# RWKV mixing plus Hadamard feed-forward layer: the first pair's recurrence items spread over three stretches, weights split ahead of W2's loads

## The chip, the cores and the metric

The kernel runs on one core of one Trainium2 chip. The metric is the device time of one execution in microseconds, the median of three; lower is better. The engines are named as in the profile: PE is the matrix engine and PEld its weight loads, DVE the vector engine, ACT the activation engine, POOL the GpSimd engine, SP the engine whose queue (SPq) issues every DMA here. They run side by side, each in program order, and meet at semaphores.

## The reference

`x` is 4 x 2048 tokens of 512 channels, float32. The kernel computes `out = x + attn(xn) + ffn(xn)` with `xn = layernorm(x)`. Cut to what matters:

```
shifted = xn one token later (zero at t = 0)
xq = mu_q * xn + (1 - mu_q) * shifted                for q in k, v, r
k, v, r = xk @ Wk.T, xv @ Wv.T, xr @ Wr.T            (512 x 512 each)
per channel, over t:  p  = max(pp, u + k_t);  e1 = exp(pp - p);   e2 = exp(u + k_t - p)
                      y  = (e1*aa + e2*v_t) / (e1*bb + e2)
                      p2 = max(w + pp, k_t);  e1b = exp(w + pp - p2);  e2b = exp(k_t - p2)
                      aa, bb, pp = e1b*aa + e2b*v_t, e1b*bb + e2b, p2      (w = -exp(wkv_w))
attn = (sigmoid(r) * y) @ Wo.T
ffn  = fwht(silu(xn @ W1.T) * (xn @ W3.T)) @ W2.T    (hidden size 2048; fwht: Walsh-Hadamard, / sqrt(2048))
```

## The kernel before

**Tiling.** The 8192 tokens are eight **pairs** `s` of two halves (a and b) of 512 tokens. Every product is done in three matmuls (high by high, low by high, high by low) on operands that were split into a high part (an ACT copy) and a low part (a subtraction). The low parts of activations are made on DVE, those of weights on POOL. The fwht is folded into W2 once, in the prologue.

**A pair** has an up stage and a down stage. The up stage is 16 steps `j`. A step makes 7 "pieces" of 6 matmuls (L852, L854, L855; a seven-product scheme for both halves and W1, W3), and from step 1 on 12 matmuls of half a's down projection (L862 to L864), 24 in steps 5, 8 and 10. The down stage is 24 steps `n`. PE runs 12 matmuls of the next pair's k, v, r product for each (L934 to L936, `r_unit` n), from n = 4 on behind 12 of half b's down projection (`down_b` n - 4). ACT and DVE at step n prepare the mixed input of `r_unit` n + 3 (L1014, L1355, L1026, L1364) and half b's hidden tile n - 1, and at n = 1 and 2 DVE empties the four accumulators of half a (`add_residual`, L1580), which `down_b` 0 needs. `turn` lies between the stages.

**The recurrence** has 8 items a pair (two halves, four channel tiles). Item w needs its k and v tile, and goes through stages 0, 1, 3, 4, 5, 6, 7 on DVE (`wkv`, L1401 on): 0 and 1 are a copy, a scan and two exponent arguments, then ACT makes two rectified and two exponentiated tiles (`rectified`, `exponentials`), 3 to 5 are products, scans and sums, 6 is a reciprocal, 7 ends in the attention tile `attf`. Items run one after the other, since the carry goes from tile half to tile half and they share `z`, `e`, `pab`, `attf`. In the up stage slot `3 j + slot` (three slots a step, `recurrence`) runs stage `divmod(3 j + slot, 8)[1]` of item 1 to 6, so 48 slots for six items, in every pair. Item 7 runs at down steps 3 to 10, the next pair's item 0 at down steps 11 to 18. In the prologue item 0 of the first pair runs around `r_unit` 8 and 9.

**DVE in an up step j**, in this order: `hidden_a(j-1)` (L1482, frees the bank of piece 5 of step j), slot 0, `gate_a_added` (L1487), `gate_b_applied` (L1496), `hidden_b` (L1501), slot 1, `hidden_a_lo` (L1464), slot 2, the next pair's `normalisation`, `b_added` (L1505, L1507), `gate_a_applied` (L1491).

**The prologue and the first pair** are special. Weights come raw from HBM into 8 slots (`load_raws`, in the order of RAWS), ACT makes their high part (`split_high`), POOL their low part (`lo`, L733), SP stores the split weights to HBM (`store_split`) for the other seven pairs. In the first pair's up stage POOL also forms the sums of W1 and W3 (L746 to L751). The prologue loads W2 in four pieces of 1 MB (`load_w2`), turns it by Hadamard matmuls within tiles after `r_unit` 8 (L966) and across tiles after `r_unit` 14 (L947), and ACT copies each turned tile. For the first pair, the token means and 1/std are laid out over partitions by matmuls of diagonals (`make_diagonal` on DVE, L1315; `spread_tokens`, L955).

Of the kernel before, what the change touches and what calls it, by code (L numbers as in the profile page):

```python
# [116 lines left out]
def build(nc, x, x_t, w_units, vectors, hadamard, out):  # L117
# [15 lines left out]
    with ctx:  # L133
# [219 lines left out]
        def _(sp):  # L353
# [145 lines left out]
            def first_half(s, j):  # L499

                if j == 0 and not is_last(s):
                    load_rows(s + 1, 0)
                if j == 1 and not is_first(s):
                    store_out(s - 1, 1)
                if not is_last(s):
                    if j in (2, 4, 6):
                        load_rows(s + 1, j // 2)
                    if 2 <= j < 2 + KT:
                        load_columns(s + 1, j - 2)
                    if j in (6, 10):  # L510
# [5 lines left out]
                if j in (11, 14):  # L516
                    store_att_b(s, (j - 11) // 3)
# [32 lines left out]
            def down_step(s, n):  # L550

                if n == 0:
                    store_hidden_b(s, FT - 1)
                    if is_first(s):
                        for i in range(HIDB):
                            load_hidden_b(s, i)
                if n == 1:
                    store_att_b(s, 2)
# [19 lines left out]
                if n == 4:  # L578
                    store_out(s, 0)
                if n == 12:  # L580
                    store_att_b(s, 3)
# [106 lines left out]
            load_raws(RAW_AT["d", 1])  # L688
# [310 lines left out]
        def _(act):  # L999
# [114 lines left out]
            def split_high(unit):  # L1114
# [18 lines left out]
                act.activation(split_place(unit)[:, 0, :], split_source(unit), ACT.Copy).then_inc(split_hi, 1)  # L1133

            def up_step(s, j):
                first = is_first(s)

                step_w, at = divmod(3 * j + 2, 8)
                starts = 2 - (at - 1) if 1 <= at <= 3 else None
                w = 1 + step_w  # L1140
                if j == 0 or j == 1:
# [57 lines left out]
            def down_step(s, n):  # L1199

                with_r, with_d = not is_last(s), not (isinstance(s, int) and s < 0)
                r = s + 1
                if with_r:
                    if n % KT == KT - 1:
                        evacuate(r, n // KT)
                    if n + MIX_AHEAD < R_UNITS:
                        mix_second(r, n + MIX_AHEAD)
                    if n + MIX_AHEAD + 1 < R_UNITS:
                        mix_first(r, n + MIX_AHEAD + 1)
                if with_d:  # L1210
                    if 1 <= n < 1 + ND:
                        hidden_b_hi(s, n - 1)
                    if n == WKV_LAST_AT + 1:
                        rectified(s, 7)
                    if n == WKV_LAST_AT + 2:
                        exponentials(s, 7)
                if with_r:
                    if with_d and n == WKV_FIRST_AT + 1:
                        rectified(r, 0)
                    if with_d and n == WKV_FIRST_AT + 2:  # L1220
                        exponentials(r, 0)
# [13 lines left out]
            split_high(("r", 2))  # L1235
            mix_second(0, 0)
            mix_second(0, 1)
            mix_first(0, 2)
            mix_second(0, 2)
            mix_first(0, 3)  # L1240
            for n in range(R_UNITS):
# [12 lines left out]
                if n == PASS_TWO_AFTER:  # L1254
                    act.wait_ge(half_stored, 16 * W2_LOADS)
                    for k, i in enumerate(TILES_TURNED):
                        act.wait_ge(w2_psum, FT + k + 1)
                        act.activation(fly[1][:, i, :], acc[i % TT][:, :], ACT.Copy).then_inc(w2_copied, 1)
                if n + 3 >= R_UNITS:
                    split_high(("u", 0, n + 3 - R_UNITS))  # L1260
# [11 lines left out]
        def _(dve):  # L1272
# [37 lines left out]
            def make_diagonal(h, a):  # L1310

                if h:
                    dve.wait_ge(spread, a + 1)
                for t in range(TT):
# [195 lines left out]
            def recurrence(s, j, slot):  # L1510

                w_item, stage = divmod(3 * j + slot, 8)
                wkv(s, 1 + w_item, stage)

# [67 lines left out]
            def down_step(s, n):  # L1582

                with_r, with_d = not is_last(s), not (isinstance(s, int) and s < 0)
                r = s + 1
                if not with_d and n == PASS_ONE_AFTER + 1:
                    for stage in range(3, 7):
                        wkv(r, 0, stage)
                if not with_d and n == 3:
                    dve.wait_ge(rstd_ready, 2)  # L1590
                    make_diagonal(1, 1)
                if with_r:
# [9 lines left out]
                if with_r:  # L1602
                    centre_at, scale_at = (CENTRE_AT, SCALE_AT) if with_d else (FIRST_CENTRE_AT, FIRST_SCALE_AT)
# [4 lines left out]
                if with_d and 0 <= n - WKV_LAST_AT < 8:  # L1608
                    wkv(s, 7, n - WKV_LAST_AT)
                if with_r:  # L1610
                    if with_d and 0 <= n - WKV_FIRST_AT < 8:
                        wkv(r, 0, n - WKV_FIRST_AT)
                    if not with_d and n == PASS_ONE_AFTER:
                        wkv(r, 0, 0)
                        wkv(r, 0, 1)
                    if not with_d and n == PASS_ONE_AFTER + 4:
                        wkv(r, 0, 7)
                    made_at, low_at = (MADE_AT, LOW_AT) if with_d else (FIRST_MADE_AT, FIRST_LOW_AT)
                    for i in made_at.get(n, ()):
# [14 lines left out]
            def first_stats(h):  # L1634
# [5 lines left out]
                add_eps(0, h)  # L1640
                dve.wait_ge(mean_copied, h + 1)
                dve.wait_ge(had_loaded, 16)
                make_diagonal(h, 0)

            first_stats(0)
            dve.wait_ge(vec_loaded, 16)
            dve.tensor_scalar(one_less_mu[:, :, :], vec[:, 0:3, :], -1.0, 1.0, ALU.mult, ALU.add)\
# [79 lines left out]
```

## Time and profile before

| | us |
|---|---|
| median of 3 runs | 2746.8 (2746.8 to 2746.91) |
| profiled execution | 2745.27, of which the span is 2743.5 |
| PE busy | 2672.6 (97%), granted clock 0.994 of full |
| DVE busy | 2204.7 (80%) |
| PEld / ACT / POOL busy | 2185.4 (80%) / 1317.5 (48%) / 238.2 (9%) |
| chain that ended last | PE 88%, DVE 8%, ACT 2%, issue 1%, DMA 1% |

All of the POOL's work and nearly all of PE's idle time lie before 404 us, in the prologue and in the first pair. A row of the timeline gives start, duration, engine, line, operation, output, inputs and, in brackets, the idle time of the engine before it and what ended it. A matmul of 512 columns starts 0.227 us after the one before it at the full clock, though its row shows a duration of 0.39.

### The profile page before, as it was taken

To read this page: it belongs to the slowest core of one execution; us is meant where nothing else is said; L and a number is where in the kernel's file an instruction comes from. 1 tells how busy PE (TensorE), PEld (TensorE's weight loads), DVE (VectorE), ACT (ScalarE), POOL (GpSimd) and SP (SyncE) were. 2 spreads that over 40 slices of the span, in tenths; PEclk is the share of its full clock that TensorE was granted. 3 is DMA by queue.
4 is the path that set the end of the run, shared out by engine and by line. 5 is a ranking of instruction groups with operands and counts; after the bars stand their busy time and mean duration, and the time that the engine had idled before them with its cause. 6 is when DMAs were issued, how large, how long until landed. Compare 5 with 4: busy or idle time off the path is not lost.

```text
span 2743.5 us, 33882 instructions
## 1 busy us (share of the span) xinstructions
PE 2672.6 (97%) x11616; PEld 2185.4 (80%) x11616; DVE 2204.7 (80%) x2970; ACT 1317.5 (48%) x2107; POOL 238.2 (9%) x180
## 2 busy tenths in 40 slices
PE   7988899999999999999999999999999999999999
PEld 4666678888888888888888888888888888888887
DVE  7698988788887888788886888878888688877785
ACT  5655456444554445444454444644455444554442
POOL 2287830000000000000000000000000000000000
PEclk9999999999999999999999999999999999999999
DMA  6787678787877878787786877878787786876777
GB/s 222 293 283 234 230 248 276 239 273 221 276 250 255 259 232 271 240 277 241 246 280 218 271 251 248 279 238 275 222 269 260 246 272 219 275 245 221 229 227 271
DMA packets 244951, 691.50 MB, mean 252 GB/s; under 512 B 31920, under 2 KB 31920, under 8 KB 244272
## 3 DMA queue, kind: packets, MB, share of 16 engines
q1 hardware_dynamic: 244784, 689.34, 76.2%
q8 instruction: 96, 1.57, 0.2%
q14 instruction: 71, 0.58, 0.1%
HBM read 575.94 MB, written 113.30 MB: 251 GB/s over the span
## 4 chain that ended last, share of the span: by engine, by line
PE 88%; DVE 8%; ACT 2%; issue 1%; DMA 1%; POOL 0%; ACTq 0%; DVEq 0%
PE gamma L852 12%; PE gamma L855 12%; PE gamma L854 12%; PE acc L862 10%; PE acc L864 10%; PE acc L863 10%; PE gamma L934 4%; PE gamma L936 4%; PE gamma L935 4%; PE alpha L852 2%; PE alpha L855 2%; PE alpha L854 2%; PE alpha L936 1%; PE alpha L935 1%; PE alpha L934 1%
## 5 line engine op out<-in xcount | busy, mean ns | idle before, releaser
L1048 ACT ACTIVATE step<-gamma 128x512 f32<-128x512 f32 x512 | 306.2, 598 | 837.8 <-PE gamma L855 814.2
L852 PE MATMUL gamma<-xs_high,wring 128*128 128x512 f32 x1280 | 502.4, 393 | 29.7 <-DVE step L1482 20.6
L855 PE MATMUL gamma<-xs_low,wring 128*128 128x512 f32 x1280 | 500.7, 391 | 0.0
L854 PE MATMUL gamma<-xs_high,wring 128*128 128x512 f32 x1280 | 500.7, 391 | 0.0
L862 PE MATMUL acc<-vring,hid 128*128 128x512 f32 x1232 | 482.0, 391 | 9.4 <-POOL vring L733 4.4
L863 PE MATMUL acc<-vring,hid 128*128 128x512 f32 x1232 | 480.0, 390 | 0.0
L864 PE MATMUL acc<-vring,hid 128*128 128x512 f32 x1232 | 479.8, 389 | 0.0
L852 PEld LDWEIGHTS gamma<-xs_high,wring 128*128 128x128 f32 x1280 | 241.7, 189 | 85.8 <-issue 22.6
L862 PEld LDWEIGHTS acc<-vring,hid 128*128 128x128 f32 x1232 | 231.9, 188 | 64.0 <-issue 11.2
L855 PEld LDWEIGHTS gamma<-xs_low,wring 128*128 128x128 f32 x1280 | 241.8, 189 | 50.8
L854 PEld LDWEIGHTS gamma<-xs_high,wring 128*128 128x128 f32 x1280 | 242.0, 189 | 49.8
L1355 DVE SCALAR_TENSOR_TENSOR step<-xt,vec,step 128x512 f32<-128x512 f32 x192 | 144.3, 755 | 160.3 <-ACT step L1014 159.5
L864 PEld LDWEIGHTS acc<-vring,hid 128*128 128x128 f32 x1232 | 231.6, 188 | 48.4
L863 PEld LDWEIGHTS acc<-vring,hid 128*128 128x128 f32 x1232 | 231.9, 188 | 47.8
L1026 ACT ACTIVATE mix<-step 128x512 fp32r<-128x512 f32 x192 | 120.6, 629 | 254.7 <-PE gamma L936 216.6
L1443 DVE RECIPROCAL z<-z 128x512 f32<-128x512 f32 x64 | 214.1, 3345 | 0.0
L934 PE MATMUL gamma<-mix,wring 128*128 128x512 f32 x522 | 203.8, 390 | 3.9 <-DVE mix L1364 3.9
L936 PE MATMUL gamma<-mix,wring 128*128 128x512 f32 x522 | 203.6, 390 | 0.0
L935 PE MATMUL gamma<-mix,wring 128*128 128x512 f32 x522 | 203.6, 390 | 0.0
L727 POOL TENSOR_TENSOR mean_rstd<-var_eps,half 128x4 f32<-128x4 f32 x16 | 22.7, 1416 | 1883.5 <-DVE var_eps L1302 1883.5
L1487 DVE TENSOR_TENSOR step<-step,alpha 128x512 f32<-128x512 f32 x128 | 86.4, 675 | 112.4 <-PE alpha L855 101.3
L1364 DVE TENSOR_TENSOR mix<-step,mix 128x512 fp32r<-128x512 f32 x192 | 139.0, 724 | 18.4 <-ACT mix L1026 9.9
(170 smaller groups left out, 4770.1 us busy)
## 6 DMA issues: line engine op xcount, KB each, us to landing
wring<-u_split SPq DMA_DIRECT2D x336, 512.0 KB, 4.3
vring<-d_split SPq DMA_DIRECT2D x288, 512.0 KB, 4.3
wring<-r_split SPq DMA_DIRECT2D x168, 512.0 KB, 4.2
raw<-spilled SPq DMA_DIRECT2D x160, 256.0 KB, 4.2
spilled<-step SPq DMA_DIRECT2D x128, 256.0 KB, 4.3
wlast<-u_split SPq DMA_DIRECT2D x112, 256.0 KB, 3.4
u_split<-wring SPq DMA_DIRECT2D x48, 512.0 KB, 3.1
res<-x SPq DMA_DIRECT2D x16, 1024.0 KB, 7.7
```

Source lines behind the costliest of these rows:

```text
L852: pe.matmul(bank[:, :], w[:, 0, col], high, start=fresh and kt == 0, stop=False, skip_group_check=True)
L854: pe.matmul(bank[:, :], w[:, 1, col], high, start=False, stop=False, skip_group_check=True)
L855: last = pe.matmul(bank[:, :], w[:, 0, col], low, start=False, stop=kt == 1, skip_group_check=True)
L862: pe.matmul(acc[tt][:, :], a[:, 0, col], w[:, 0, :], start=first, stop=False)
L863: pe.matmul(acc[tt][:, :], a[:, 1, col], w[:, 0, :], start=False, stop=False)
L864: return pe.matmul(acc[tt][:, :], a[:, 0, col], w[:, 1, :], start=False, stop=final)
L934: pe.matmul(bank[:, :], w[:, 0, col], m_in[:, 0, :], start=kt == 0, stop=False)
L935: pe.matmul(bank[:, :], w[:, 1, col], m_in[:, 0, :], start=False, stop=False)
L936: last = pe.matmul(bank[:, :], w[:, 0, col], m_in[:, 1, :], start=False, stop=kt == KT - 1)
L1048: act.activation(to, bank[:, :], ACT.Copy).then_inc(u_copied, 1)
L1355: dve.scalar_tensor_tensor(f, xt[:, kt, 1 + h * N:1 + (h + 1) * N], vec[:, q, kt:kt + 1], f, ALU.mult, ALU.add).then_inc(mix_full, 1)
L1443: dve.reciprocal(z[:, 1, :], z[:, 1, :]).then_inc(wkv_step, 1)
```

## The change

What it does, in six parts:

1. Up stage of the first pair only: the slot table becomes FIRST_UP_WKV. It holds stage 7 of item 1 and all of items 2 to 5, 34 slots of 48, with free slots between. The other pairs' tables give the same order as before.
2. Down stage of the first pair: FIRST_DOWN_WKV runs item 6 at n = 0 to 6, item 7 at n = 7 to 13, the next pair's item 0 at n = 15 to 22. The next pair's `centre` and `scale` move from n = 3 to 6 to n = 4 to 7, the stores of attention tiles of half b to j = 12 and n = 0, 8, 14.
3. Prologue: item 1 is run too; stages 0 and 1 at `r_unit` step 13, stages 3 to 6 at step 15 ahead of that step's mixing, its ACT work among the copies of W2's second turn.
4. ACT in the first pair rectifies and exponentiates where the new tables have stage 1, always in slot 1 or 2.
5. Raw k, v, r weights: all 12 loads are issued ahead of W2's four loads (the last four wait for a freed slot). ACT splits them two at a time: r3 to r5 before the first `r_unit`, r6 to r11 by step 2.
6. The second half's diagonals are made by eight ACT copies with a scale at step 1, no longer by DVE; their matmuls come after `r_unit` 4 in place of 3.

```diff
-WKV_LAST_AT, WKV_FIRST_AT = 3, 11
+UP_WKV = {k: (1 + k // 8, k % 8) for k in range(3 * FT)}
+FIRST_UP_WKV = {2: (1, 7)}
+FIRST_UP_WKV |= {k: (2, i) for i, k in enumerate((3, 5, 6, 8, 9, 11, 13, 15))}
+FIRST_UP_WKV |= {16 + i: (3, i) for i in range(8)}
+FIRST_UP_WKV |= {k: (4, i) for i, k in enumerate((24, 25, 27, 28, 30, 31, 33, 34))}
+FIRST_UP_WKV |= {k: (5, i) for i, k in enumerate((36, 37, 39, 40, 42, 43, 45, 46))}
+DOWN_WKV = {3 + i: ((7, i),) for i in range(8)} | {11 + i: ((8, i),) for i in range(8)}
+FIRST_DOWN_WKV = {0: ((6, 0), (6, 1)), 2: ((6, 3),), 3: ((6, 4),), 4: ((6, 5),), 5: ((6, 6),), 6: ((6, 7),),
+                  7: ((7, 0), (7, 1)), 9: ((7, 3),), 10: ((7, 4),), 11: ((7, 5),), 12: ((7, 6),), 13: ((7, 7),),
+                  15: ((8, 0),), 16: ((8, 1),), 18: ((8, 3),), 19: ((8, 4),), 20: ((8, 5),), 21: ((8, 6),),
+                  22: ((8, 7),)}
+RECTIFY_AT, EXP_AT = {4: 7, 12: 8}, {5: 7, 13: 8}
+FIRST_RECTIFY_AT, FIRST_EXP_AT = {0: 6, 7: 7, 16: 8}, {1: 6, 8: 7, 17: 8}
-SPREAD_AFTER, PASS_ONE_AFTER, PASS_TWO_AFTER = 3, 8, 14
+SPREAD_AFTER, PASS_ONE_AFTER, PASS_TWO_AFTER = 4, 8, 14
...
             load_columns_first(0)
-            load_raws(2)
+            load_raws(4)
             load_rows_first(2)
             load_rows_first(3)
-            load_raws(4)
-            load_w2(0)
+            load_raws(RAW)
             load_columns_first(1)
-            load_raws(6)
-            load_w2(1)
-            load_raws(RAW)
-            load_w2(2)
-            load_w2(3)
+            load_raws(12)
+            for i in range(W2_LOADS):
+                load_w2(i)
...
+            def diagonals_b(a):
+                if a:
+                    act.wait_ge(rstd_ready, 2)
+                else:
+                    act.wait_ge(mean_copied, 2)
+                act.wait_ge(spread, 2)
+                for t in range(TT):
+                    act.activation(diagonal[:, a, t, :], had[:, 2, :], ACT.Copy, scale=mean_rstd[:, 1, a, t:t + 1])\
+                        .then_inc(diagonal_made, 1)
...
             for n in range(R_UNITS):
                 down_step(-1, n)
-                if n + 3 < 12:
-                    split_high(("r", n + 3))
+                if n < 3:
+                    split_high(("r", 6 + 2 * n))
+                    split_high(("r", 7 + 2 * n))
+                if n == 1:
+                    diagonals_b(0)
+                    diagonals_b(1)
...
-                if not with_d and n == PASS_ONE_AFTER + 1:
+                if not with_d and n in (PASS_ONE_AFTER + 1, PASS_TWO_AFTER + 1):
                     for stage in range(3, 7):
-                        wkv(r, 0, stage)
-                if not with_d and n == 3:
-                    dve.wait_ge(rstd_ready, 2)
-                    make_diagonal(1, 1)
+                        wkv(r, int(n > PASS_TWO_AFTER), stage)
```

## Rows read from the trace of the kernel before

**Rows 1.** Busy time by engine in stretches (busy, instructions; clock, DMA share, GB/s).
```profile
128.98:380.03 251.05, 216.41 (x888) 170.94 (x889) 227.59 (x238) 127.36 (x220) 191.37 (x143) 0.96 0.71 246
...
404.00:510.00 106.00, 105.98 (x468) 87.76 (x468) 81.21 (x105) 53.96 (x85) 0.00 (x0) 1.00 0.78 253
510.00:711.00 201.00, 201.00 (x888) 166.42 (x887) 168.69 (x240) 90.11 (x143) 2.86 (x2) 1.00 0.78 254
```

**Rows 2.** PE's waits, 128.98 to 404 us: for whom, total us, times, longest.
```profile
PE gamma L852 <- DVE step L1482: 20.6, 7, 5.3
PE acc L862 <- POOL vring L733: 4.4, 3, 1.7
PE gamma L852 <- ACT step L1048: 4.2, 4, 2.4
PE gamma L852 <- POOL wring L733: 4.0, 4, 1.7
PE gamma L934 <- DVE mix L1364: 3.9, 1, 3.9
```

**Rows 3.** PE's timeline: its longest stalls in the first pair (idle time in brackets).
```profile
180.82 0.47 PE L852 MATMUL gamma<-xs_high,wring 128*128 128x512 f32 x1 [2.40 <-ACT step L1048]
...
208.74 0.77 PE L852 MATMUL gamma<-xs_high,wring 128*128 128x512 f32 x1 [3.61 <-DVE step L1482]
209.30 0.63 PE L854 MATMUL gamma<-xs_high,wring 128*128 128x512 f32 x1
...
258.69 0.77 PE L852 MATMUL gamma<-xs_high,wring 128*128 128x512 f32 x1 [5.27 <-DVE step L1482]
...
344.14 0.77 PE L852 MATMUL gamma<-xs_high,wring 128*128 128x512 f32 x1 [5.18 <-DVE step L1482]
...
386.89 0.47 PE L934 MATMUL gamma<-mix,wring 128*128 128x512 f32 x1 [3.85 <-DVE mix L1364]
```

**Rows 4.** DVE's timeline: the recurrence's first item, in the prologue.
```profile
55.05 0.16 DVE L1417 COPY pab<-carry 128x3 f32<-128x3 f32 x1
...
66.80 0.69 DVE L1427 TENSOR_TENSOR z<-e,kvr 128x512 f32<-128x512 f32 x1 [8.96 <-ACT e L1095]
...
73.15 3.35 DVE L1443 RECIPROCAL z<-z 128x512 f32<-128x512 f32 x1
...
85.58 0.69 DVE L1457 SCALAR_TENSOR_TENSOR attf<-kvr,z 128x512 f32<-128x512 f32 x1
```

**Rows 5.** DVE's timeline: `hidden_a` that opens and that follows up step 7.
```profile
239.36 0.69 DVE L1482 TENSOR_TENSOR step<-step,gamma 128x512 f32<-128x512 f32 x1
...
257.86 0.69 DVE L1482 TENSOR_TENSOR step<-step,gamma 128x512 f32<-128x512 f32 x1
```

**Rows 6.** Groups by line and form, DVE, 129 to 380 us (POOL at work).
```profile
L1501 DVE TENSOR_TENSOR step<-step 128x512 f32<-128x512 f32 x15 | 14.5, 967 | 1.6
```

**Rows 7.** The same group in the second pair, 510 to 711 us (POOL idle).
```profile
L1501 DVE TENSOR_TENSOR step<-step 128x512 f32<-128x512 f32 x15 | 10.4, 692 | 1.6
```

**Rows 8.** Busy time as in Rows 1, of up steps 2 and 7 alone.
```profile
155.80:170.33 14.53, 12.93 (x55) 10.09 (x56) 14.32 (x17) 6.45 (x12) 12.15 (x10) 1.00 0.90 311
...
235.43:248.48 13.05, 12.62 (x56) 10.02 (x56) 12.91 (x13) 7.08 (x13) 12.97 (x10) 1.00 1.00 359
```

**Rows 9.** Timelines of PE, DVE: around the turns of W2 in the prologue.
```profile
50.76 1.75 DVE L1364 TENSOR_TENSOR mix<-step,mix 128x512 fp32r<-128x512 f32 x1
...
53.70 15.70 PE L966 MATMUL acc<-fly,had 128*128 128x512 f32 x32 [3.33 <-DVE xt L1341]
...
105.68 0.75 DVE L1355 SCALAR_TENSOR_TENSOR step<-xt,vec,step 128x512 f32<-128x512 f32 x1 [15.54 <-ACT step L1014]
```

**Rows 10.** DVE's timeline: down steps 1 and 2 of the first pair.
```profile
398.35 0.75 DVE L1355 SCALAR_TENSOR_TENSOR step<-xt,vec,step 128x512 f32<-128x512 f32 x1 [4.45 <-ACT step L1014]
...
403.28 1.28 DVE L1580 TENSOR_TENSOR res<-res,acc 128x512 f32<-128x512 f32 x2
```

**Rows 11.** DVE's waits, 404 to 510 us.
```profile
DVE step L1355 <- ACT step L1014: 16.0, 13, 3.2
```

More of the change, by code:

```diff
@@ L515, in first_half @@
                     load_residual(s, 0)
-                if j in (11, 14):
+                if j == 12 if is_first(s) else j in (11, 14):
                     store_att_b(s, (j - 11) // 3)
@@ L556, in down_step @@
                             load_hidden_b(s, i)
-                if n == 1:
+                if n == 0 and is_first(s):
+                    store_att_b(s, 1)
+                if n == (8 if is_first(s) else 1):
                     store_att_b(s, 2)
@@ L579, in down_step @@
                     store_out(s, 0)
-                if n == 12:
+                if n == (14 if is_first(s) else 12):
                     store_att_b(s, 3)
@@ L1133, in split_high @@
                 act.activation(split_place(unit)[:, 0, :], split_source(unit), ACT.Copy).then_inc(split_hi, 1)
+            def diagonals_b(a):
[7 more added lines that the diff above has]
+                        .then_inc(diagonal_made, 1)
             def up_step(s, j):
                 first = is_first(s)
-                step_w, at = divmod(3 * j + 2, 8)
-                starts = 2 - (at - 1) if 1 <= at <= 3 else None
-                w = 1 + step_w
+                starts = w = None
+                for slot in range(3):
+                    item, stage = (FIRST_UP_WKV if first else UP_WKV).get(3 * j + slot, (0, 0))
+                    if stage == 1:
+                        starts, w = slot, item
                 if j == 0 or j == 1:
@@ L1212, in down_step @@
                         hidden_b_hi(s, n - 1)
[L1213 to L1216, printed above, removed]
+                    rectify_at, exp_at = (FIRST_RECTIFY_AT, FIRST_EXP_AT) if is_first(s) else (RECTIFY_AT, EXP_AT)
+                    for at, what in ((rectify_at, rectified), (exp_at, exponentials)):
+                        if at.get(n) == 8:
+                            if with_r:
+                                what(r, 0)
+                        elif n in at:
+                            what(s, at[n])
                 if with_r:
[L1218 to L1221, printed above, removed]
                     high_at = HIGH_AT if with_d else FIRST_HIGH_AT
@@ L1236, in _ @@
             mix_second(0, 0)
+            split_high(("r", 3))
             mix_second(0, 1)
             mix_first(0, 2)
+            split_high(("r", 4))
             mix_second(0, 2)
             mix_first(0, 3)
+            split_high(("r", 5))
             for n in range(R_UNITS):
                 down_step(-1, n)
-                if n + 3 < 12:
-                    split_high(("r", n + 3))
+                if n < 3:
[4 more added lines that the diff above has]
+                    diagonals_b(1)
                 if n == PASS_ONE_AFTER:
@@ L1258, in _ @@
                         act.activation(fly[1][:, i, :], acc[i % TT][:, :], ACT.Copy).then_inc(w2_copied, 1)
+                        if k == 3:
+                            rectified(0, 1)
+                        if k == 9:
+                            exponentials(0, 1)
                 if n + 3 >= R_UNITS:
@@ L1310, in make_diagonal @@
             def make_diagonal(h, a):
-                if h:
-                    dve.wait_ge(spread, a + 1)
                 for t in range(TT):
@@ L1510, in recurrence @@
             def recurrence(s, j, slot):
-                w_item, stage = divmod(3 * j + slot, 8)
-                wkv(s, 1 + w_item, stage)
+                at = FIRST_UP_WKV if is_first(s) else UP_WKV
+                if 3 * j + slot in at:
+                    wkv(s, *at[3 * j + slot])
             def normalisation(r, j):
@@ L1602, in down_step @@
                 if with_r:
-                    centre_at, scale_at = (CENTRE_AT, SCALE_AT) if with_d else (FIRST_CENTRE_AT, FIRST_SCALE_AT)
+                    late = not with_d or is_first(s)
+                    centre_at, scale_at = (FIRST_CENTRE_AT, FIRST_SCALE_AT) if late else (CENTRE_AT, SCALE_AT)
                     if n in centre_at:
@@ L1607, in down_step @@
                         scale(r, 1, scale_at[n])
-                if with_d and 0 <= n - WKV_LAST_AT < 8:
-                    wkv(s, 7, n - WKV_LAST_AT)
+                if with_d:
+                    for item, stage in (FIRST_DOWN_WKV if is_first(s) else DOWN_WKV).get(n, ()):
+                        if item < 8:
+                            wkv(s, item, stage)
+                        elif with_r:
+                            wkv(r, 0, stage)
                 if with_r:
-                    if with_d and 0 <= n - WKV_FIRST_AT < 8:
-                        wkv(r, 0, n - WKV_FIRST_AT)
                     if not with_d and n == PASS_ONE_AFTER:
@@ L1617, in down_step @@
                         wkv(r, 0, 7)
+                    if not with_d and n == PASS_TWO_AFTER - 1:
+                        wkv(r, 1, 0)
+                        wkv(r, 1, 1)
                     made_at, low_at = (MADE_AT, LOW_AT) if with_d else (FIRST_MADE_AT, FIRST_LOW_AT)
@@ L1640, in first_stats @@
                 add_eps(0, h)
-                dve.wait_ge(mean_copied, h + 1)
-                dve.wait_ge(had_loaded, 16)
-                make_diagonal(h, 0)
             first_stats(0)
+            dve.wait_ge(mean_copied, 1)
+            dve.wait_ge(had_loaded, 16)
+            make_diagonal(0, 0)
             dve.wait_ge(vec_loaded, 16)
```

## The prediction

> **What bounds the kernel now.** I read the stretches first. In the second pair's up stage 888 matmuls take 201 us and PE has no idle time; the first pair runs the same 888 in 251.05, with PE busy for 216.41 and the granted clock at 0.96; its down stage, 404 to 510, has no gap left [rows 1]. So what PE loses lies before 404 us, and whatever PE wins there moves the end by as much. At 0.2266 us a matmul the up stage would take 201.2, so 49.8 us are lost in it. PE's waits name them [rows 2]: 20.6 for DVE's L1482 in 7 waits, 8.4 for POOL's weight splits, 4.2 for ACT's copies, and 3.9 for DVE's mixing at the turn. The rest is clock: after each of the longest stalls [rows 3] matmuls start 0.43 us apart (209.30 is such a one) for a while before they come back to 0.227. Summing what start to start exceeds 0.2266, that cost 2.6 us after the stall at 208.74, 1.6 after 258.69, 1.3 after 293.29, 1.7 after 344.14 and 1.7 after 386.89.
>
> The reader is to see why L1482 is late. It is the first DVE instruction of step j and frees the bank of PE's fourth piece. DVE is busy for 227.59 of 251.05 us [rows 1]. From one L1482 to the next in step 7 it works 18.5 us without a gap [rows 5], against 54 matmuls or 12.24 us of PE. Two things fill it: recurrence stages (5, 6 and 7 of an item here), and POOL, beside which a 0.692 us instruction takes 0.967 [rows 6, 7].
>
> **Up stage, the recurrence.** An item is 15 DVE instructions with 14.3 us between them (first, one of the middle and last in [rows 4]), 13.7 with the overlap at each handover. By that timeline stages 0 and 1 take 1.35 each, 3 and 4 1.8, 5 2.4, 6 3.3 and 7 1.4. Before, 6 items or 82 us lie in the 16 steps; after, 4 items and a stage 7, or 56. What counts is where. The seven stalls for L1482 come at j = 2, 3, 5, 8, 10, 12 and 13 (those at 5, 8 and 13 stand in [rows 3], the one at 10 is like them), most behind a heavy step. Slot by slot, recurrence work goes at j = 1 from 6.1 to 2.7, at 2 from 6.2 to 1.8, at 4 from 7.6 to 3.3, at 9 from 6.1 to 1.8, at 12 from 7.6 to 2.7. Steps 5 to 8 keep what they had (7.1 at j = 7), and j = 3, 11 and 14 get more (by 1.2, 1.6 and 0.7). PE needs L1482 about 4.8 us into the step, which is the slack. So I take away the stalls at j = 2 and 3 (0.4 and 0.9), 5 (3.6), 10 (3.9), 12 (1.4) and 13 (5.2): 15.4 us, with 5.6 of clock behind 5, 10 and 13. The one at j = 8 (5.27 and 1.6 of clock) I leave: before step 6 DVE already waits for PE, so its lateness at 8 grows inside steps 6 and 7, which the change does not touch.
>
> **ACT.** The stall of 2.40 at 180.82 [rows 3] is an ACT copy queued behind `rectified`, which waited 3.4 us for DVE's stage 1. The new table has no stage 1 in slot 0, so ACT never takes it up early in a step; with the one of 1.2 before it, whose cause is DVE's lateness in step 2, 3.6 us go.
>
> **Turn.** The stall of 3.85 at 386.89 with 1.7 of clock [rows 3] comes from DVE's lateness in step 15, which loses stage 5 (3.1 as it ran there). Pairs without it show no wait. 5.6 go.
>
> **POOL** works 191.37 us in these 16 steps [rows 1], 12.0 a step, nearly what PE needs (12.6). Where PE stood still for DVE, POOL caught up; that cover goes. The 8.4 us of waits on it are bounded by none left (gain 8.4) and by 12 steps that last as long as step 2, 14.5 us, in place of about 13.3, near step 7 [rows 8], the common length of steps without a DVE stall (loss 14.4). I take a loss of 2, near the common length, since DVE also asks for less beside it. What DVE and POOL do to each other is 0.967 against 0.692 [rows 6, 7]. The Trainium skill says of this (SBUF — State Buffer, Who interferes with whom) that a vector instruction with two SBUF inputs and a GpSimd instruction that reads SBUF exclude each other for the whole instruction. By that rule each removed two-input stage frees POOL as well; this is the rival "more goes" below, and the sum stands without it.
>
> **Down stage.** Item 6 adds 13.7 us of DVE between n = 0 and 6. DVE waits 16.0 us for ACT there in 13 waits [rows 11] and is busy 81 of 106 [rows 1], so the sum fits. The start does not quite: stages 0 and 1 fit into the idle 4.45 before 398.35 [rows 10], but ACT's two rectified tiles (1.9 us) then stand ahead of the mix of n = 1 and its two exponentials (2.0) ahead of the mix of n = 2. DVE's `add_residual` pair, now at 403.28 [rows 10], comes some 2.4 later, and `down_b` 0 waits for it with 0.25 to spare now. Bounds: 0, and 3.9 if all of ACT's work shows. I take 2.1. Queued behind on SP: stores of attention tiles at n = 0, 8 and 14, a step or more after their stage 7, so SP does not stand.
>
> **Prologue.** Splits done early on ACT and POOL take POOL's share out of DVE's chain to `scale` (the 1.75 at 50.76 against 0.69 [rows 9], four such), which ends PE's wait of 3.33 at 53.70. Against it, `r_unit` 4 follows 3 directly, without the diagonals' matmuls to cover the copying of four banks, and ACT gets there behind eight diagonals and four splits. I see `r_unit` 5 start where it did and the turn start between 0 and 3 us earlier; I take 2. Diagonals leave DVE (1.7 us), covered by the same wait. W2's loads leave SP some 12 us later, are needed at 53.70, and 4 MB at the 246 GB/s of [rows 1] take 17 us, so they land by 44; cost 0, and one for one beyond 53.7. Item 1: stages 3 to 6 are 9.6 us of DVE that start when ACT's exponentials end, near 99, in the idle 15.54 before 105.68 [rows 9]. They reach to 108, 2.5 beyond; DVE has 1 us of idle from there to the first pair's start, so that is 1.5 later. Bounds 0 and 2.5. Together 0.5 gained, between 3 gained and 2.5 lost.
>
> **The sum.** 15.4 + 5.6 + 3.6 + 5.6 + 0.5 - 2 - 2.1 = 26.6 us. The profiled execution took 2745.27 (1.8 of it outside the span), so 2718.7; the median of the runs lies 1.5 above it, so **2720.2**.
>
> **The rivals.**
> - The split chain sets the pace: PE runs ahead, and POOL, or the transfers behind it, end each step. For: step 7 at 13.05 us had POOL busy 12.97 and the DMA share at 1.00 [rows 8]. Against: it was still just 0.8 above 12.24. With the 14.4 us worked out above in place of 2: 2732.6. Chance 0.23.
> - More goes: the stall at j = 8 too (6.9) and half of POOL's waits, as DVE and POOL hinder each other less. For: [rows 6, 7]. Against: steps 6 and 7 are untouched. 26.6 + 6.9 + 2 + 4 = 39.5 less: 2707. Chance 0.17.
> - Nothing comes of it: the DMA engines, at 0.71 of their time over the stage [rows 1] and full in step 7, already hold it at 246 GB/s, and PE waits for raw weights instead of DVE. 2746. Against: no wait of PE or of ACT's splits ends in a load. Chance 0.05.
> - Slower: DVE never catches up in the first down stage, since its idle time there (16.0 [rows 11]) is ACT's lateness and cannot be used. It decides if the delay of n = 2 comes again in each of the 20 steps: 2.1 x 20 = 42 lost against 28.7 won, 2760. Against: a step there lasts 5.44 us and mixing is three ahead. Chance 0.03.
>
> **How the numbers follow.** The forecast has 0.52. The range takes in the first two rivals with their unknown terms, 2705 to 2735, and leaves the other two out. About 0.2%, 5.5 us, is what a measurement can tell from no change: faster 0.92, same 0.05, slower 0.03.
>
> **What would show it.** Right: PE's waits for DVE's L1482 fall to one long one of 5 us, at j = 8; none of 3 us at the turn; up stage 223 to 228 us long; POOL's waits as now or somewhat more; a new PE wait for L1580 near the start of the down stage; the first pair starts within 2 us of 128.98; the second pair's up stage still 201. Wrong: more than 15 us of waits for POOL, waits for loads, or new L1482 stalls at j = 12 or 15.

## The result, and the profile after

The changed kernel took **2727.5 us** (2726.2 to 2728.8) against 2746.9 of the kernel before beside it: ratio 0.9929, 95% interval 0.9917 to 0.9941. The forecast was 2720.2, its range 2705 to 2735. The gain is 19.4 us where 26.6 were forecast, so the direction and the range held and 7.2 us of the gain are missing. The profiled execution has a span of 2724.8 us. Because lines moved, the old L1482 is now L1514, L852 L863, L862 L873, L1048 L1059, L733 L744, L934 L945, L1364 L1396, L1580 L1613, L1505 L1537; the high split on ACT is L1144.

Busy time by engine in four stretches of the changed kernel, columns as in [rows 1]: the up stage of the first pair; from its end to the first matmul of the next `r_unit`; from there to the second pair; the second pair's up stage.

```profile
129.95:359.60 229.65, 209.60 (x888) 167.65 (x889) 211.09 (x216) 119.66 (x211) 193.75 (x143) 0.98 0.77 266
359.60:363.86 4.26, 3.05 (x14) 2.23 (x13) 4.26 (x7) 3.61 (x6) 1.69 (x1) 1.00 0.91 350
363.86:493.60 129.74, 125.02 (x547) 102.25 (x547) 106.05 (x138) 68.75 (x107) 0.00 (x0) 1.00 0.75 252
...
505.00:706.00 201.00, 201.00 (x888) 166.38 (x887) 171.41 (x244) 87.25 (x141) 2.86 (x2) 1.00 0.80 257
```

The same cuts of the kernel before:

```profile
380.03:386.89 6.86, 3.01 (x12) 2.17 (x13) 6.86 (x11) 2.65 (x5) 1.70 (x1) 1.00 0.66 242
386.89:512.95 126.06, 125.81 (x547) 103.63 (x548) 93.54 (x123) 65.63 (x104) 0.00 (x0) 0.99 0.77 253
```

The ledger from these rows: the first pair starts 1.0 us later (129.99 against 128.98), the up stage is 21.4 shorter (251.05 in [rows 1], 229.65 here), the turn 2.6 shorter, and the same 547 matmuls of the down stage and the last step before the second pair take 3.7 longer. Sum 19.3. From there on the two kernels are nearly alike: the second pair's up stage is 201.00 in both, and the whole spans differ by 18.7. Two other cuts are used below. Between PE's first matmul into `alpha` in step 0 and the one in step 15, "from `alpha` to `alpha`", the up stage took 236.1 before and 217.0 now; from the latter to the second pair's first `alpha` it took 145.1 in both.

PE's waits in the changed kernel, 127 to 400 us (for whom, total us, times, longest), to be read against [rows 2]:

```profile
PE gamma L863 <- DVE step L1514: 8.3, 4, 5.2
PE acc L873 <- POOL vring L744: 6.7, 3, 3.6
PE acc L873 <- DVE res L1613: 3.6, 2, 1.9
PE gamma L863 <- POOL wring L744: 2.9, 4, 1.6
PE gamma L863 <- ACT step L1059: 2.0, 3, 1.4
...
PE gamma L945 <- DVE mix L1396: 1.2, 1, 1.2
PE gamma L945 <- DMA wring<-r_split: 0.8, 1, 0.8
```

The wait for `hidden_a` fell from 20.6 to 8.3. Those for POOL rose from 8.4 to 9.6, and the one for `add_residual` went from 0.25 in one wait to 3.6 in two. PE's timeline of the changed kernel has them in place; after none of them but the two at 215 and 248 does the clock fall for longer than a few matmuls:

```profile
215.09 0.71 PE L873 MATMUL acc<-vring,hid 128*128 128x512 f32 x1 [3.55 <-POOL vring L744]
...
248.79 0.76 PE L863 MATMUL gamma<-xs_high,wring 128*128 128x512 f32 x1 [5.22 <-DVE step L1514]
...
363.86 0.47 PE L945 MATMUL gamma<-mix,wring 128*128 128x512 f32 x1 [1.21 <-DVE mix L1396]
...
380.57 0.47 PE L873 MATMUL acc<-vring,hid 128*128 128x512 f32 x1 [1.77 <-DVE res L1613]
...
384.03 0.50 PE L873 MATMUL acc<-vring,hid 128*128 128x512 f32 x1 [1.85 <-DVE res L1613]
```

The one at 248.79 is the stall of step 8 that the prediction left in place; in [rows 3] it is the one at 258.69. The one at 215.09 is new, and the wait is put down to POOL. ACT's and POOL's timelines show who was late:

```profile
208.70 1.06 ACT L1100 ACTIVATE e<-z 128x1024 f32<-128x1024 f32 x1 [2.80 <-DVE z L1455]
209.67 1.04 ACT L1101 ACTIVATE e<-z 128x1024 f32<-128x1024 f32 x1
210.62 1.99 ACT L1106 ACTIVATE e<-e 128x1024 f32<-128x1024 f32 x2
212.51 0.57 ACT L1059 ACTIVATE step<-gamma 128x512 f32<-128x512 f32 x1
212.99 1.13 ACT L1144 ACTIVATE vring<-raw 128x512 fp32r<-128x512 f32 x2
```

```profile
210.14 1.02 POOL L738 TENSOR_TENSOR mean_rstd<-var_eps,half 128x4 f32<-128x4 f32 x1 [0.31 <-DVE var_eps L1336]
213.68 2.51 POOL L744 TENSOR_TENSOR vring<-raw,vring 128x512 fp32r<-128x512 f32 x2 [2.52 <-ACT vring L1144]
```

ACT waits 2.80 us at the rectified tiles of item 3, whose stage 1 DVE has only just made, then does the two rectified and two exponentiated tiles, and the split of the next `vring` tiles stands behind. POOL, idle for 2.52, cannot form the low part before that, and PE waits for it. So "waits for POOL" is here a wait for ACT's queue, and through it for DVE. Item 3's stage 1 stands in the same slot as in the kernel before, slot 2 of step 5; there PE had just stood 3.61 us for DVE [rows 3], ACT took item 3's tiles up without a wait at 217.11, and PE's wait for the next `vring` was 1.35.

### The profile page after: what moved, and what is told of

Its sections match the earlier page's. It is cut to its first block, busy times and chain, and to the rows that moved or that the text cites. A ratio compares the mean times of both kernels' runs of the same rounds, so it can differ in the third digit from the quotient of the medians.

```text
span 2724.8 us, 33882 instructions
## 1 busy us (share of the span) xinstructions
PE 2665.6 (98%) x11616; PEld 2181.7 (80%) x11616; DVE 2205.9 (81%) x2962; ACT 1318.0 (48%) x2115; POOL 243.0 (9%) x180
## 4 chain that ended last, share of the span: by engine, by line
PE 87%; DVE 8%; ACT 2%; issue 2%; DMA 1%; POOL 1%; SPq 0%; ACTq 0%; DVEq 0%
PE gamma L863 12%; PE gamma L865 12%; PE gamma L866 12%; PE acc L873 10%; PE acc L875 10%; PE acc L874 10%; PE gamma L945 4%; PE gamma L947 4%; PE gamma L946 4%; PE alpha L866 2%; PE alpha L865 2%; PE alpha L863 2%; PE alpha L946 1%; PE alpha L947 1%; PE alpha L945 1%
## 5 line engine op out<-in xcount | busy, mean ns | idle before, releaser
L1059 ACT ACTIVATE step<-gamma 128x512 f32<-128x512 f32 x512 | 305.7, 597 | 840.9 <-PE gamma L866 817.9
L863 PE MATMUL gamma<-xs_high,wring 128*128 128x512 f32 x1280 | 500.2, 391 | 14.2 <-DVE step L1514 8.3
L873 PE MATMUL acc<-vring,hid 128*128 128x512 f32 x1232 | 481.5, 391 | 14.2 <-POOL vring L744 6.7
L863 PEld LDWEIGHTS gamma<-xs_high,wring 128*128 128x128 f32 x1280 | 240.9, 188 | 69.3 <-issue 11.2
L873 PEld LDWEIGHTS acc<-vring,hid 128*128 128x128 f32 x1232 | 231.3, 188 | 68.9 <-issue 14.8
L1387 DVE SCALAR_TENSOR_TENSOR step<-xt,vec,step 128x512 f32<-128x512 f32 x192 | 144.4, 756 | 145.3 <-ACT step L1025 144.6
L945 PE MATMUL gamma<-mix,wring 128*128 128x512 f32 x522 | 204.0, 391 | 7.0 <-ACT kvr L1052 3.5
L1396 DVE TENSOR_TENSOR mix<-step,mix 128x512 fp32r<-128x512 f32 x192 | 135.9, 708 | 18.8 <-DMA spilled<-step 9.5
```

The costliest lines, as they stand in the source:

```text
L863: pe.matmul(bank[:, :], w[:, 0, col], high, start=fresh and kt == 0, stop=False, skip_group_check=True)
L873: pe.matmul(acc[tt][:, :], a[:, 0, col], w[:, 0, :], start=first, stop=False)
L945: pe.matmul(bank[:, :], w[:, 0, col], m_in[:, 0, :], start=kt == 0, stop=False)
L1059: act.activation(to, bank[:, :], ACT.Copy).then_inc(u_copied, 1)
L1387: dve.scalar_tensor_tensor(f, xt[:, kt, 1 + h * N:1 + (h + 1) * N], vec[:, q, kt:kt + 1], f, ALU.mult, ALU.add).then_inc(mix_full, 1)
```

## The experiments

**1. Which part carries the gain.** The recurrence tables alone, with the prologue's loads, splits and diagonals as before:

```diff
-            load_raws(4)
+            load_raws(2)
             load_rows_first(2)
             load_rows_first(3)
-            load_raws(RAW)
+            load_raws(4)
+            load_w2(0)
...
-                if n == 1:
-                    diagonals_b(0)
-                    diagonals_b(1)
```

> The recurrence part alone: the new tables of the first pair, item 1 in the prologue, the new stores; raw loads, splits and diagonals of the prologue as in the kernel before. Theory (the gain is the up stage's, from DVE's load per step): nearly the whole gain, 2728 to 2731 us, the up stage (first alpha piece of step 0 to that of step 15) at 217 us as with both parts. Rival (the prologue part carries a gain of its own of 5 us or more): 2733 or above.

Measured: 2728.1 (2726.3 to 2729.1), ratio 0.9935, interval 0.9918 to 0.9951, as the theory said. The up stage took 218.6 from `alpha` to `alpha`, and both long stalls of the changed kernel are there, 3.55 for `vring` and 5.28 for `hidden_a`. The other half, the prologue alone with the old tables:

```diff
-UP_WKV = {k: (1 + k // 8, k % 8) for k in range(3 * FT)}
-FIRST_UP_WKV = {2: (1, 7)}
+WKV_LAST_AT, WKV_FIRST_AT = 3, 11
...
-                if not with_d and n in (PASS_ONE_AFTER + 1, PASS_TWO_AFTER + 1):
+                if not with_d and n == PASS_ONE_AFTER + 1:
```

> The prologue part alone: k, v, r weights loaded and split ahead, diagonals of the second half on ACT, spread after r_unit 4; the recurrence as in the kernel before. Theory: PE starts W2's first turn about 1.2 us earlier (52.5 against 53.7) and, without item 1 behind W2's second turn, the first pair 1 to 3 us earlier; up stage 236 us as before; 2744 to 2746 us. Rival (the parts need each other): no gain or a loss, 2747 or above, since the copy of four banks behind r_unit 3 stalls PE by 3.5 us.

Measured: 2743.8 (2742.1 to 2745.0), ratio 0.9992, interval 0.9982 to 1.0001: no difference from the kernel before that the runs can tell. PE waits seven times for `hidden_a`, 18.8 us in all, as before; the first pair's pieces on the `alpha` bank begin at 128.25 in place of 131.68. In the whole change they begin at 131.46, with the tables alone at 134.61. So the tables carry the gain. The prologue's loads, splits and diagonals together win 3.2 to 3.4 us up to this point, and item 1's work there costs 2.9 to 3.2: together 0.2.

**2. The stall at 215.** Stages 0 and 1 of item 3, and with them the last of item 2, go one slot earlier, so that stage 1 is made sooner; stages 3 to 7 stay:

```diff
-FIRST_UP_WKV |= {k: (2, i) for i, k in enumerate((3, 5, 6, 8, 9, 11, 13, 15))}
-FIRST_UP_WKV |= {16 + i: (3, i) for i in range(8)}
+FIRST_UP_WKV |= {k: (2, i) for i, k in enumerate((3, 5, 6, 8, 9, 11, 13, 14))}
+FIRST_UP_WKV |= {k: (3, i) for i, k in enumerate((15, 16, 18, 19, 20, 21, 22, 23))}
```

> The changed kernel, with stage 7 of item 2 one slot earlier (step 4, slot 2), stages 0 and 1 of item 3 one slot earlier each (step 5, slots 0 and 1); stages 3 to 7 of item 3 stay. Theory (the new stall of 3.55 us for POOL's vring at 215 is ACT, which at the end of step 5 waits 2.8 us for the exponent arguments and then makes four tiles ahead of the weight split): that stall falls under 1 us, 2 to 3.5 us faster than the changed kernel, and the stall of 5.2 us at step 8 stays. Rival (POOL's own rate sets it): the stall at 215 stays within 1 us.

Measured: 2727.6 (2722.7 to 2730.9), ratio 0.9931, interval 0.9915 to 0.9948. Timelines of PE and ACT:

```profile
200.73 0.47 PE L863 MATMUL gamma<-xs_high,wring 128*128 128x512 f32 x1 [1.17 <-DVE step L1514]
...
215.24 0.47 PE L873 MATMUL acc<-vring,hid 128*128 128x512 f32 x1 [1.35 <-POOL vring L744]
...
207.62 1.06 ACT L1100 ACTIVATE e<-z 128x1024 f32<-128x1024 f32 x1 [0.22 <-DVE z L1455]
```

ACT's wait for item 3 fell from 2.80 to 0.22, and 3.55 became 1.35, the wait that the kernel before had there. So ACT's lateness made the other 2.2. The forecast was under 1 for the stall and 2 to 3.5 us for the kernel; neither came. A wait of 1.17 appeared ahead of it, in step 5, which got 1.4 us longer. Steps 5 and 6 together still got 2.3 shorter, of which 1.7 is lower clock behind the old stall. Over the whole stage, 216.6 from `alpha` to `alpha`, it is 0.4: steps 7, 10 and 11 came out longer and step 13 shorter, and the last three did so in a second execution of the changed kernel too (experiment 4).

**3. The stall at step 8.** As in 2, and stages 3 to 6 of item 3 also one slot earlier, so that step 7 loses stage 5 to step 6 and keeps 6 and 7:

```diff
-FIRST_UP_WKV |= {k: (3, i) for i, k in enumerate((15, 16, 18, 19, 20, 21, 22, 23))}
+FIRST_UP_WKV |= {k: (3, i) for i, k in enumerate((15, 16, 17, 18, 19, 20, 21, 23))}
```

> As s1_early, and stages 3, 4 and 5 of item 3 in step 6, stage 6 and 7 in step 7, so that step 7 has 4.7 us of recurrence in place of 7.1. Theory (the stall at step 8 is DVE's load inside step 7): the stall of 5.2 us for L1514 with its 1.9 us of slow clock falls under 2 us, and the kernel is 5 to 10 us faster than the changed one, 2718 to 2723. Rival (DVE and POOL are both full over steps 6 to 8, so the lateness only moves): stall of 4 us or more at step 7 or 8, under 4 us gained.

Measured: 2723.5 (2720.3 to 2724.0), ratio 0.9917, interval 0.9901 to 0.9934. The forecast was 2718 to 2723, and its rival wanted a stall of 4 us or more and under 4 us gained; the result lies between them, 4.0 us under the changed kernel by the medians. The four times, at most 2724.0, lie below all eight that the changed kernel took here and in experiment 4, at least 2726.2. The 5.22 at step 8 is gone, and in PE's timeline one of half its size stands a step earlier:

```profile
232.10 0.49 PE L863 MATMUL gamma<-xs_high,wring 128*128 128x512 f32 x1 [2.50 <-DVE step L1514]
```

The up stage took 212.2 from `alpha` to `alpha`, 4.8 us less. Of the three kernels of experiment 4 with the same tables, two took 212.2 and 212.3 and one 215.7, so how much of the 4.8 is the order's is known only roughly. Some of DVE's lateness in steps 6 to 8 was a matter of order; what is left moved.

**4. The start of the down stage.** On top of 3, item 6's ACT work goes to n = 2 and 3, past the two `add_residual`, item 7 and the stores follow, and item 1's ACT work in the prologue comes earlier among the turned tiles:

```diff
-FIRST_RECTIFY_AT, FIRST_EXP_AT = {0: 6, 7: 7, 16: 8}, {1: 6, 8: 7, 17: 8}
+FIRST_RECTIFY_AT, FIRST_EXP_AT = {2: 6, 8: 7, 16: 8}, {3: 6, 9: 7, 17: 8}
...
-                        if k == 3:
+                        if k == 2:
                             rectified(0, 1)
-                        if k == 9:
+                        if k == 6:
                             exponentials(0, 1)
```

> s7_light with two more edits. One: item 6's rectified and exponentiated tiles at down steps 2 and 3 in place of 0 and 1, its stages 3 to 7 at 4 to 8, item 7 at 8 to 14, stores a step later. Two: item 1's ACT work in the prologue behind tiles 2 and 6 of W2's second turn, in place of 3 and 9. Theory (the two stalls of 1.8 us for L1613 come from ACT making those tiles ahead of the mixing of down steps 1 and 2): both fall under 0.5 us and the stretch from the first pair's last up step to the second pair's first shrinks from 145 to 141 to 143 us. Theory (the stalls of 1.6 and 2.1 us for ACT in the prologue come from stages 3 to 6 of item 1 reaching 2.5 us into the mixing): the first pair starts 1 to 2.5 us earlier. Sum: 3 to 5 us under s7_light. Rival: DVE's work in the down stage is what binds, the same 13.7 us, so the stretch stays at 145.

Measured: 2721.3 (2717.8 to 2721.7), ratio 0.9901, interval 0.9885 to 0.9918. This is 2.2 under experiment 3 where 3 to 5 were forecast, with intervals that overlap. The two waits of 1.8 for `add_residual` are gone, so item 6's early work was their cause (the edit moves its ACT tiles and, with them, DVE's stages 3 to 7), and PE waits for a weight load instead:

```profile
423.43 0.47 PE L873 MATMUL acc<-vring,hid 128*128 128x512 f32 x1 [3.38 <-DMA vring<-d_split]
```

From step 15's `alpha` to the second pair's it took 144.8, where 141 to 143 were forecast. I took the store of item 6's attention tile on SP for the cause, where SP had stood 5.5 us. Three kernels on one chip: the changed one again, the same edits with that store at n = 11 in place of 9, and this without the prologue's edit.

```diff
-                if n == (9 if is_first(s) else 1):
+                if n == (11 if is_first(s) else 1):
                     store_att_b(s, 2)
```

> The changed kernel itself once more, beside the two variants, for a direct comparison on one chip. Theory: 2726 to 2729, and the first pair's start, which lay 1.5 us earlier in the run with three edits than in the changed kernel already at W2's first turn, shows how much of such a difference is from run to run: first turn at 51 to 52.5. Rival (the edits bring the early first turn): 52.4 to 52.5 here and 51 in the two variants.

> The three edits again (item 3 without a gap before stage 7, item 6 later in the down stage, item 1's ACT work earlier in the second turn), and the store of item 6's attention tile at n = 11 in place of 9. Theory (SP stood 5.5 us at that store, and a weight load behind it came 3.4 us late): the wait of 3.4 near 423 goes, nothing takes its place, since ACT no longer stands before the mix of n = 1; from the last up step to the second pair 141 to 142.5 in place of 144.8; 2717 to 2720. Rival (DMA has no room there whatever the order on SP: the loads of the down stage took 4.6 to 5.8 us each at a share near 1): a wait of 2 us or more for another load, the stretch stays above 144, 2721 or more.

> The same without the edit of the prologue: item 1's ACT work stands where the changed kernel has it. Theory: waits of 1.6 and 2.1 us are back ahead of the last mixed inputs, and the first pair starts 0.5 to 1.5 us later, counted from W2's first turn, because the wait of 2.6 for xs_low falls to 1.4 when these come; 2718 to 2721. Rival (the wait for xs_low takes all of it): the same start within 0.3, and no difference in time.

Measured: the changed kernel 2728.8 (2727.0 to 2730.8); with the later store 2723.0 (2717.9 to 2725.7), ratio to the kernel before 0.9910, interval 0.9893 to 0.9926; without the prologue's edit 2724.3 (2720.0 to 2725.4), ratio 0.9917, interval 0.9900 to 0.9933. Both gain on the changed kernel beside them, by 5.8 and 4.5 us of the medians, about as much as experiment 3 alone. The down stage gave nothing: the stretch from step 15's `alpha` to the second pair's, forecast at 141 to 142.5, took 145.3 and 148.2, and 143.8 in the changed kernel beside them. The store was not the cause. The wait is still there, with 2.44 and 3.18 us. The timelines of ACT, DVE, SP and PE in the kernel with the later store suggest why:

```profile
411.25 1.06 ACT L1100 ACTIVATE e<-z 128x1024 f32<-128x1024 f32 x1 [6.78 <-DVE z L1455]
...
415.37 0.75 DVE L1387 SCALAR_TENSOR_TENSOR step<-xt,vec,step 128x512 f32<-128x512 f32 x1 [3.02 <-ACT step L1025]
416.04 0.68 DVE L1396 TENSOR_TENSOR mix<-step,mix 128x512 fp32r<-128x512 f32 x1
416.64 0.69 DVE L1507 TENSOR_TENSOR hid<-raw,hid 128x512 fp32r<-128x512 f32 x1
...
410.86 0.32 SPq L437 DMA_DIRECT2D vring<-d_split  x1
417.36 0.32 SPq L466 DMA_DIRECT2D raw<-spilled  x1
417.77 0.38 SPq L395 DMA_DIRECT2D wring<-r_split  x1
418.20 0.42 SPq L505 DMA_DIRECT2D res<-x  x1
418.68 0.50 SPq L458 DMA_DIRECT2D spilled<-attf  x1
419.29 0.38 SPq L437 DMA_DIRECT2D vring<-d_split  x1
...
427.38 0.77 PE L873 MATMUL acc<-vring,hid 128*128 128x512 f32 x1 [2.44 <-DMA vring<-d_split]
```

It looks like the mechanism of 215 once more. ACT stands 6.78 us at item 7's rectified tiles, since DVE made stage 1 behind the reciprocal of item 6; the scaled copy for DVE's mixing is queued behind, so the low part of the hidden tile (L1507) comes late; SP, which may load the next one only then, stands 6.2 us from 411.18 to 417.36; and the loads that follow leave in a bunch, with 1 MB of residual ahead of the weights. In the changed kernel SP stands 4.2 there and the weights leave before the residual. All this is read from timelines: no kernel moved item 7's ACT work to test it, and the last step is read from the order on SP alone, since none moved the residual's load.

For the prologue's edit the waits of 1.6 and 2.1 us before 118 went and 2.55 came in place of 1.41 at the first piece, yet from W2's first turn to the first pair's `alpha` pieces it took 76.6 and 76.7 us in the two kernels with the edit and 79.0 in the changed kernel (twice), in experiment 3's and in the one without the edit. That is 2.4, more than either theory allowed. It is no proof: two other kernels without the edit, whose prologue is the changed kernel's, took 79.8 (experiment 2) and 77.3 (the second of experiment 5). Between 2723.0 and 2724.3 the runs can't tell either. The early first turn (51 in place of 52.5) that came with the first of these kernels came in one without the edit too, so it is no effect of it.

**5. What sets the pace of the up stage.** One kernel makes POOL's sums of W1 and W3 on 8 of 256 columns from step 1 on; another runs stages 3 to 6 of items 2 to 5 on DVE on 8 of 512 columns.

```diff
-                near, far = slice(0, C // 2), slice(C // 2, C)
+                L = C // 2 if j == 0 else 8
+                near, far = slice(0, L), slice(C // 2, C // 2 + L)
```

> The changed kernel with POOL's sums of W1 and W3 made on 8 of 256 columns from step 1 on, so those weight units are not right: some 3 to 5 of POOL's 12 us a step are gone. Rival (POOL sets the pace of the up stage): the up stage of 217 us falls to 208 or less, the stall at step 8 halves. Theory (DVE's load per step sets it, POOL adds about 7 us of waits): the waits for POOL vanish, the stall at step 8 stays at 4 us or more, the up stage is 209 to 213 us. Beside it, DVE instructions with two SBUF inputs should come nearer to their 0.69 us.

```diff
+                L = 8 if is_first(r) and 2 <= w_item <= 5 else N
...
-                    dve.tensor_tensor(z[:, 0, :], e_one[:, 0, :], v, ALU.mult)
+                    dve.tensor_tensor(z[:, 0, 0:L], e_one[:, 0, 0:L], v[:, 0:L], ALU.mult)
```

> The changed kernel with stages 3 to 6 of items 2 to 5 in the first pair made on 8 of 512 columns (that part of the attention is not right): some 37 us of DVE's work leave the up stage. Theory: every wait for DVE's L1514 vanishes and POOL's chain is what is left, up stage 205 to 209 us against 201 without any loss, with POOL's waits at 3 to 8 us. Rival (POOL or the transfers bind already): the up stage stays above 212 us.

Measured, a single run each: 2708.0 and 2706.1. The first pair's up stage, by engine, of the first and of the second kernel:

```profile
130.20:343.00 212.80, 204.53 (x889) 167.66 (x890) 193.95 (x217) 118.26 (x211) 148.22 (x143) 0.99 0.82 288
```

```profile
126.40:338.60 212.20, 204.93 (x889) 165.85 (x890) 179.63 (x219) 119.87 (x211) 181.54 (x144) 1.00 0.85 298
```

With POOL's sums short the stage of 229.65 us was 16.9 shorter, with DVE's items short 17.4. Each alone ends about the same part of the 28.4 us that the stage loses against 201.2. Both keep three waits for `vring`, 4.0 us in all; with POOL light one of 4.0 for `hidden_a` at step 8 stays, with DVE light 1.4 in two waits, and 1.6 for `wring`. Look at the other engine's column too: with POOL's sums short DVE, whose instructions had not changed, was busy 193.95 us in place of 211.09; with the items short POOL, likewise unchanged, 181.54 in place of 193.75. Each engine's work lengthens the other's.

From `alpha` to `alpha`, the cut of the first expectation, the stage fell from 217.0 to 200.3 with POOL light. The theory had 209 to 213 there, since it held that POOL's work is worth only its own waits, and it failed. The rival's 208 or less came, though the stall at step 8 shrank only from 5.2 to 4.0 where the rival had it halved. With DVE light the whole stage took 212.2 where 205 to 209 were forecast; the rival had more than 212. Each of the two is one execution.

## Why the prediction was right, and where it was off

The forecast's direction, place and range were right. Its up stage of 223 to 228 us was not met, by 1.7 us (229.65), and its terms fared so:

- **Recurrence, waits for L1482: 15.4 forecast, 12.3 measured.** The large ones (3.6, 3.9, 5.2 at j = 5, 10, 13) are gone or small, and step 8 kept its 5.2 as forecast. Off by 3.1: 0.7, 0.7 and 1.6 stayed at 10, 12 and 13. A likely reason, not tested by itself: the slack of 4.8 us was compared with slot work at its price in [rows 4], where POOL was idle; beside POOL a stage of two-input instructions costs more (1.79 and 1.77 us for the last two of stage 1 at 205.18 and 206.89, 0.75 each at 373.25 and 373.92).
- **ACT: 3.6 forecast, 2.2 measured** in the wait named ACT, and **the new stall of 3.55 at step 6** takes that away again. This is the step that failed. I argued that stage 1, now never in slot 0, is never taken up early by ACT. But in slot 2 of step 5, where the kernel before had it too, it can still be late, and what stands behind it on ACT is not only PSUM copies but the splits that POOL and PE need. Before, PE's own stall for DVE in that step hid this. Experiment 2 shows the cause, for 2.2 of the 3.55.
- **POOL: a loss of 2 forecast, 1.2 measured** in waits (8.4 to 9.6), of which 2.2 are ACT's lateness by experiment 2. The size held by luck, for another reason than mine.
- **Clock: 5.6 + 1.7 forecast to come back.** Both did, and the mean granted clock of the stage rose from 0.96 to 0.98. Two things were not forecast and cancel: 1.7 us of matmuls 0.43 apart behind the new stall at 215.09, and 1.6 that the kernel before lost so at the stage's start, where its wait for `xs_low` was 2.59 and is now 1.41.
- **Turn: 5.6 forecast.** The stall fell by 2.6, from 3.85 to 1.21, and the 1.7 of clock went too: 4.3. DVE is less late in step 15, not in time.
- **Down stage: a loss of 2.1 forecast, 3.7 measured** in the ledger, and 5.4 with the clock of the turn that came back inside the same stretch. The mechanism and the place are as forecast (ACT's four tiles ahead of two mixes, then `add_residual`), but PE waited for each of its two instructions, 1.77 and 1.85; I had taken the delay once. The upper bound of 3.9 would have been the better value. A wait of 0.76 for a weight load at 375.77 is in the 5.4 as well.
- **Prologue: 0.5 gained forecast, 0.2 gained measured**, from +3.4 and -3.2 where I had +2 and -1.5. `r_unit` 4 waits 3.46 us for ACT's copies, as its queue of diagonals and splits suggested.
- **The sum** is 7.2 us short: by the ledger the up stage gave 21.4 where 22.6 were forecast for it, the turn 2.6 and the stretch behind it -3.7 where together 3.5 were forecast, the start -1.0 where +0.5 was (at the `alpha` pieces it is +0.2, since the kernel before began them at the lower clock). That is 1.2 + 4.6 + 1.5. In the second execution of the changed kernel (experiment 4) the stretch from step 15's `alpha` to the second pair's took 143.8 in place of 145.1 and the up stage 218.2 in place of 217.0, so terms of about 1 us are within what two executions differ by.
- **The rivals.** The split chain as sole pace setter did not come: POOL waits stayed at 9.6. "More goes" did not either: the 5.2 at step 8 stayed. But experiment 5 shows that what the two rivals argue from is one thing: DVE and POOL lengthen each other. The Trainium skill (SBUF — State Buffer, Who interferes with whom) has the rule that a vector instruction with two SBUF inputs and a GpSimd instruction that reads SBUF exclude each other; the rows below agree. The slower rival did not come: the down stage lost its delay once and from 404 on PE had 89.27 busy of 89.60. Nor did transfers hold the stage: PE's waits for loads came to 0.8 us before 400, at a DMA share of 0.77, and the shorter stages of experiment 5 had 0.82 and 0.85.

## What to carry to other kernels

Where engines run in order, read a wait's releaser back through its queue: two stalls here (POOL's at 215, `add_residual`) had one cause, an ACT instruction for the recurrence queued early, with urgent copies behind it, and a third (the weight load at 423) reads the same. Put such an instruction where its input is already there, not where its result would be nice to have. When two engines that slow each other are both nearly full, as DVE and POOL here at 92% and 84% of the stage, try to take work off either one, and don't price it by that engine's own waits. Moving work within DVE also won something here (experiment 3), though part of a stall that it removed came back elsewhere.

## What the runs showed of the hardware

How tightly DVE and POOL exclude each other. DVE's timeline of the changed kernel around 208, beside POOL, which by its own rows is busy to 209.82 and has nothing to do from 211.16 to 213.68:

```profile
206.89 1.77 DVE L1455 SCALAR_TENSOR_TENSOR z<-kvr,vec,pab 128x512 f32<-128x512 f32 x1
208.59 1.26 DVE L1332 COPY mean_rstd<-mean_var 128x4 f32<-128x4 f32 x1
209.89 0.17 DVE L1336 TENSOR_SCALAR var_eps<-mean_var 128x4 f32<-128x4 f32 x1
...
211.16 0.67 DVE L1537 TENSOR_TENSOR step<-step 128x512 f32<-128x512 f32 x1
```

```profile
206.38 3.44 POOL L744 TENSOR_TENSOR wring<-sums,wring 128x512 fp32r<-128x512 f32 x2
```

A copy of four columns lasted 1.26 us and ended within 0.03 us of POOL's tile. In the kernel before the same copy ran while POOL had nothing to do, from 210.96 to 216.77:

```profile
216.66 0.16 DVE L1298 COPY mean_rstd<-mean_var 128x4 f32<-128x4 f32 x1
```

The copy has one input, so it is no case of the rule named above for two; these rows show only that it waited. Afterwards instructions are back at 0.67. Not all are hit. By groups (131 to 345 us), DVE's add of two SBUF tiles averaged 1061 ns in the first pair's up stage and 692 in the second's, while the reciprocal and the instruction that reads PSUM did not change:

```profile
L1533 DVE TENSOR_TENSOR step<-step 128x512 f32<-128x512 f32 x14 | 14.9, 1061 | 1.5
L1475 DVE RECIPROCAL z<-z 128x512 f32<-128x512 f32 x3 | 10.0, 3343 | 0.0
L1519 DVE TENSOR_TENSOR step<-step,alpha 128x512 f32<-128x512 f32 x15 | 10.1, 673 | 8.4 <-PE alpha L866 8.2 <-ACT step L1059 0.2
```

Small shifts in time seem to decide who gets in first: two kernels of experiment 4 with the same instructions in the up stage took 212.2 and 215.7 us for it (from `alpha` to `alpha`), and DVE's instructions part at the same subtraction into `hid` in step 0 (0.69 and 1.14 us). In the first it started 0.07 us before POOL's sum, in the second 0.15 after one. That such a difference grows to 3.5 us is an observation of two executions, not a tested cause. It does set how finely two schedules of this stage can be told apart.
